# The second layer's first two units: sums of squares and scores placed behind the next projection, the adapters' mean in one piece

## The reference

```python
x = x + tanh(g_xattn[0]) * L0_attention(layernorm(x), ctx)     # rotary, masked, 32 heads, 8 key groups
x = x + tanh(g_ffn[0])   * L0_experts(layernorm(x))            # 16 experts, top 2
x = x + tanh(g_xattn[1]) * L1_attention(layernorm(x), ctx)
x = x + tanh(g_ffn[1])   * L1_lora(layernorm(x))               # 4 adapters, top 2
```

```python
q = rmsnorm(hidden @ Wq.T) * q_norm_w
k = rmsnorm(ctx @ Wk.T) * k_norm_w
probs = softmax(q @ k.T / sqrt(128) + mask)
out = (probs @ v) @ Wo.T
```

## Time and profile before

| | us |
|---|---|
| median of three executions (lowest, highest) | 1195.96 (1195.57, 1196.04) |
| the profiled execution | 1196.31 |
| its span, first to last instruction | 1194.3 |
| TensorE busy | 1181.7 |
| VectorE busy | 829.7 |
| GpSimd busy | 580.6 |
| ScalarE busy | 424.0 |

### The profile page before, as it was taken

One profiled execution on the slowest core, in us unless ns is written; L12 is line 12 of the kernel. 1 busy time (PEld: TensorE's weight loads), 2 busy tenths in 40 slices (PEclk: granted clock), 3 DMA queues, 4 the chain that ended last, 5 costly groups with the idle time before them and its releaser, 6 DMA issues.

```text
span 1194.3 us, 16826 instructions
## 1 busy us (share of the span) xinstructions
PE 1181.7 (99%) x6178; PEld 944.8 (79%) x6178; DVE 829.7 (69%) x1454; ACT 424.0 (36%) x746; POOL 580.6 (49%) x396
## 2 busy tenths in 40 slices
PE   9999999999999999999999999999999999999998
PEld 7888888777777777777788888777777777777776
DVE  4656546888888888788984335766676767657795
ACT  5145152222213222222452124535443443544432
POOL 5522533766767576676463112335354554545500
PEclk9999999999999999999999999999999999999999
DMA  7844635712212221211211003111221221211201
GB/s 282 261 145 167 201 117 161 281 54 80 80 53 72 86 79 44 79 45 45 97 63 36 1 1 138 50 49 71 86 82 44 79 78 54 70 53 40 76 1 72
DMA packets 57314, 106.54 MB, mean 89 GB/s; under 512 B 3632, under 2 KB 36528, under 8 KB 51888
## 3 DMA queue, kind: packets, MB, share of 16 engines
q1 hardware_dynamic: 56736, 104.82, 25.4%
q0 software_dynamic: 384, 1.05, 0.2%
q10 hardware_dynamic: 144, 0.00, 0.0%
HBM read 78.59 MB, written 27.26 MB: 89 GB/s over the span
## 4 chain that ended last, share of the span: by engine, by line
PE 91%; DVE 6%; POOL 2%; issue 1%; ACT 0%; DVEq 0%; POOLq 0%
PE ps_q L225 13%; PE ps_b L225 13%; PE ps_b L227 13%; PE ps_b L226 13%; PE ps_q L227 12%; PE ps_q L226 12%; PE ps_s L935 4%; PE ps_b L962 4%; PE ps_q L922 1%; PE ps_s L273 1%; PE ps_q L2039 1%; PE ps_b L469 1%; PE ps_s L1730 1%; PE ps_q L519 0%; DVE x_sb L1439 0%
## 5 line engine op out<-in xcount | busy, mean ns | idle before, releaser
L225 PE MATMUL ps_q<-hT_hi,wq_hi 128*128 128x512 f32 x512 | 206.3, 403 | 0.0
L226 PE MATMUL ps_q<-hT_lo,wq_hi 128*128 128x512 f32 x512 | 199.8, 390 | 0.0
L227 PE MATMUL ps_q<-hT_hi,wq_lo 128*128 128x512 f32 x512 | 199.4, 389 | 0.0
L225 PE MATMUL ps_b<-wo_hi,o_hi 128*128 128x512 f32 x440 | 171.5, 390 | 0.6 <-POOL wo_lo L1253 0.6
L226 PE MATMUL ps_b<-wo_lo,o_hi 128*128 128x512 f32 x440 | 171.2, 389 | 0.0
L227 PE MATMUL ps_b<-wo_hi,o_lo 128*128 128x512 f32 x440 | 171.2, 389 | 0.0
L1428 DVE TENSOR_TENSOR o_lo<-ps_b,o_hi 128x512 fp32r<-128x512 f32 x128 | 82.0, 683 | 63.7 <-ACT o_hi L1138 62.4
L225 PEld LDWEIGHTS ps_q<-hT_hi,wq_hi 128*128 128x128 f32 x512 | 96.0, 188 | 33.2 <-issue 11.2
L1260 POOL TENSOR_TENSOR qT<-q_t 128x512 f32<-128x512 f32 x64 | 89.7, 1402 | 65.8 <-DVE q_t L1363 60.0
L1439 DVE SCALAR_TENSOR_TENSOR x_sb<-ps_b,gates,x_sb 128x512 f32<-128x512 f32 x117 | 83.8, 723 | 43.6 <-PE ps_b L227 43.2
L728 POOL TENSOR_TENSOR wq_lo<-wq_raw,wq_hi 128x512 fp32r<-128x512 f32 x64 | 90.3, 1414 | 47.8 <-ACT wq_hi L722 47.8
(11 more groups left out here) (272 smaller groups left out, 2474.6 us busy)
## 6 DMA issues: line engine op xcount, KB each, us to landing
wq_raw<-in_wq SPq DMA_DIRECT2D x16, 1024.0 KB, 4.8
wo_raw<-in_wo SPq DMA_DIRECT2D x16, 1024.0 KB, 4.8
kT<-kT_spill SPq DMA_DIRECT2D x32, 256.0 KB, 3.9
v_hi<-v_hi_spill SPq DMA_DIRECT2D x16, 512.0 KB, 3.7
v_lo<-v_lo_spill SPq DMA_DIRECT2D x16, 512.0 KB, 4.6
v_hi_spill<-vs_hi SPq DMA_DIRECT2D x12, 512.0 KB, 5.4
v_lo_spill<-vs_lo SPq DMA_DIRECT2D x12, 512.0 KB, 6.7
kw_raw<-in_wk SPq DMA_DIRECT2D x4, 1024.0 KB, 7.1
```

The costliest lines, as they stand in the source:

```text
L225: nc.tensor.matmul(dst, l_hi, r_hi, start=first, stop=False)
L226: nc.tensor.matmul(dst, l_hi, r_lo, start=False, stop=False)
L227: return nc.tensor.matmul(dst, l_lo, r_hi, start=False, stop=last)
```

## The change

In the second layer's steps (0, 1) and (1, 0) (`opening`), TensorE makes the first projection of the step and only then the sums of squares and the scores of the unit before. In step (0, 1) a wait for the last low part of the layernormed x is put ahead of that projection. `square_sums` of unit 1 thereby moves from the end of step (0, 1) into step (1, 0), behind `project(1, 0, 0)`. The mean of the adapters' weights is made with four matmuls in one piece at the end of step (0, 1). On ScalarE the first query of unit 1 goes ahead of the norms of unit 0. On VectorE the turn of the sums of unit 1 moves from step (0, 1), where it stood ahead of the low part of unit 0's probabilities, to step (1, 0), behind it.

```diff
--- before.py
+++ after.py
@@ -1012,15 +1012,18 @@
                     for t in range(PAIRS):
                         project_out(0, 0, 0, t)
                     return
-                if second_first_scores(lay, g, h):
-                    lora_mean_pe(pe, True)
-                if do_score and lay:
-                    if not (isinstance(g, int) and (g, h) == (1, 0)):
-                        square_sums(us, 1 - h)
+                opening = lay and isinstance(g, int) and (g, h) in ((0, 1), (1, 0))
+                if do_score and lay and not opening:
+                    square_sums(us, 1 - h)
                     score(us, 1 - h, g if h else g - 1)
                 at_first = lay and isinstance(g, int) and (g, h) == (0, 0)
+                if second_first_scores(lay, g, h):
+                    pe.wait_ge(*lns[2]("lo", NT))
                 if do_project:
                     project(g, h, 0)
+                if opening:
+                    square_sums(us, 1 - h)
+                    score(us, 1 - h, g if h else g - 1)
                 if do_score and lay == 0:
                     score(us, 1 - h, g if h else g - 1)
                 if do_project:
@@ -1038,8 +1041,7 @@
                     project(g, h, 3)
                 for t in range(PAIRS):
                     if second_first_scores(lay, g, h) and t == 1:
-                        lora_mean_pe(pe, False)
-                        square_sums(us + 1, 1)
+                        lora_mean_pe(pe)
                     if do_finish:
                         project_out(up, h, g - 1, t)
 
@@ -1172,9 +1174,9 @@
                 if do_finish and h == 0 and not (isinstance(g, int) and g == 1):
                     for j in range(J):
                         wo_high(g - 1, j)
-                query_ahead = do_score and do_project and lay and h == 0 and not (isinstance(g, int) and g == 1)
+                query_ahead = do_score and do_project and lay and (h == 0 or second_first_scores(lay, g, h)) and not (isinstance(g, int) and g == 1)
                 if query_ahead:
-                    queries(uq, 0, 0)
+                    queries(uq, h, 0)
                 if do_score and lay:
                     norms(us)
                 for j in range(J):
@@ -1477,7 +1479,6 @@
                     sums(us)
                     att_normalise(dve, lay, us)
                     turn_probs(us)
-                    turn_sums(us + 1, h)
                     att_probs_low(dve, lay, us)
                     return
                 if lay == 0 and isinstance(g, int) and (g, h) == (0, 0):
@@ -1512,7 +1513,7 @@
                     return
                 rotated(0)
                 if do_score:
-                    if lay and not (isinstance(g, int) and (g, h) == (1, 0)):
+                    if lay:
                         turn_sums(us, 1 - h)
                     turn_scores(us, 1 - h)
                     if lay:
@@ -1998,15 +1999,13 @@
 
             return att[1]("y_added", 2 * (G - 1) * PAIRS + i + 1)
 
-        def lora_mean_pe(pe, first):
-
-            if first:
-                pe.wait_ge(lora["a_in"], 16)
-                pe.wait_ge(moe["gu"], 2 * NT)
-            for k in range(2) if first else range(2, KC):
+        def lora_mean_pe(pe):
+
+            pe.wait_ge(lora["a_in"], 16)
+            pe.wait_ge(moe["gu"], 2 * NT)
+            for k in range(KC):
                 last = nc.tensor.matmul(ps_b[0][:, 0:LN], ones[:, :], a_raw[:, k, :], start=k == 0, stop=k == KC - 1)
-            if not first:
-                last.then_inc(lora["a_sum"], 1)
+            last.then_inc(lora["a_sum"], 1)
 
         def lora_mean_act(act):
```

## The result

The change made the kernel slower: 1203.0 us (median of six executions, 1201.19 to 1203.75) against 1195.64 us for the kernel before (six executions, 1195.24 to 1196.04). The ratio is 1.0058, with a 95% interval of 1.0049 to 1.0068. It is 7.4 us over the kernel before, where the forecast has 5.8 (1201.8 less 1195.96). The profiled execution is the fastest one (1201.19 us, span 1199.4 us); the other five took 1202.56 to 1203.75 us. The mean granted clock over the whole span was 0.999 of full speed in the fastest one and 0.997 in each of the other five.

A forecast was written before the change was run, and what follows sets the result against it. TensorE, busy 1181.7 of 1194.3 us, was taken as the bound. Opening waits put it 4.1 us behind, then 5.8 with the late transpose, giving 1201.8 us from a median of 1195.96; range 1198.7 to 1203.2.

The forecast's parts named there:

- First gap: Before unit 1's first projection: TensorE waits for ScalarE's Copy to free the bank; 0.57 us cost, 1.4 us wait.
- The chain's start: Unit 0's softmax: sums end 3.32 us later, VectorE's eight copies take 1.40 us, transposed scores start 2.9 us later.
- The port: Unit 0's scaling or mask addition on VectorE is held by a GpSimd query-weight subtraction: 1.2 us, bounds 0 and 1.3.
- The exponential and P(2.0): Late exponential delays unit 1's last queries on ScalarE; unit 2's first projection waits 3.3 us, TensorE 4.1 us behind.
- P(2.0) at full rate: Unit 2's first projection, behind the new wait, was taken to run at full clock in 2.75 us.
- the fall of the clock: Rival: after the 3.3 us wait, TensorE drops from 2.4 to 1.2 GHz; 1202.9 or 1205.7 us; chance 0.12.
- The rival's smaller price: Clock-fall rival with only unit 2's first projection slow (5.5 us, 1.7 hidden): 1.1 us more, 1202.9 us.
- The second new wait: Before unit 2's second projection: wait for VectorE's transpose of unit 1's sums, 778.1 to 779.85 us; 5.8 us behind.
- After that: After unit 2's second projection: unit 0's values find probabilities ready; later work shifts 5.5 to 5.9 us, nothing regained.
- Ports shared without waiting: Rival: VectorE and GpSimd operations run together; 3.0 us behind, 1198.9 us; chance 0.20 for sharing in part or whole.
- Bank waits only: Rival: exponential not late for ScalarE, only bank waits cost: 1.1 us, 1197.1 us; chance 0.07.
- Not slower if the bank were another: Rival: without waiting for the Copy, both 0.29 us waits vanish: 1195.4 us; chance 0.05 for a gain or nothing.

The follow-up runs named there:

- no_port: The change with GpSimd's four low-part query-weight subtractions held until unit 0's shift is done: 1201.35 us, 5.5 over the kernel before.
- second_alone: Kernel before with only the second place changed (unit 2's first projection ahead of unit 1's sums and scores; their turn behind probabilities' low part): 1196.66 us, 1.0 over.
- exp_last: The change with unit 0's exponential moved in ScalarE's queue from ahead of unit 1's query 2 to behind query 3: 1203.47 us, 7.6 over the kernel before.
- change_again: The changed kernel itself, unaltered, measured once more as a yardstick: 1202.17 us, 6.5 over the kernel before.
- fill_wait: The change with 12 unread matmuls behind the mean, in TensorE's long wait: 1201.9 us, 6.2 over the kernel before.
- first_alone: Kernel before with only the first place changed (unit 1's first projection ahead of unit 0's sums and scores): 1199.32 us, 3.6 over.
- fill_turn: The change with 12 unread matmuls in TensorE's long wait and VectorE's turn of unit 1's sums back ahead of the probabilities' low part: 1200.17 us, 4.2 over before.
- own_bank_turn: The change with first projections of units 1 and 2 in a free bank and unit 1's sums turned ahead of unit 0's normalisation: 1199.13 us, 3.3 over before.
- own_bank: The change with the first projections of units 1 and 2 put into a free PSUM bank: 1202.45 us, 6.6 over the kernel before.
- bank_second: Kernel before with only the second place changed, its projection in a free bank, sums turned before probabilities' low part, whole mean in first gap: 1194.71 us against 1196.01.

## Why the prediction was right, and where it was not

*First gap.* Predicted: a wait of 1.4 us for the Copy. Measured: 1.36. The transpose of the sums was hidden behind the scores, as stated. The sums were done 5.25 us behind the Square (751.90 to 757.15) against 4.96 predicted: P(1.0) took 2.93 us and not 2.75, and started 0.1 later.

*The chain's start.* The eight copies took 1.43 us (1.40 predicted; 1.79 before).

*The port.* Predicted: 1.2 us, by rows of shorter operations. Measured: 1.07, on the scaling itself, the second of the two orders named. The scaling ended 1.09 us after GpSimd did, and takes 1.23 alone. The Trainium skill's page "SBUF — State Buffer" (section "SBUF: two separate sides") calls the shared port pair an exclusive lock; the trace agrees within 0.14 us. The normalisation was held too, 2.02 us instead of 1.23 (the prediction had it start later and run alone). no_port shows the price by itself; it shows that the two operations do not run side by side, not what they share.

*The exponential and P(2.0).* Predicted 15.7 and 19.5 us behind the Square, with 3.3 us of waiting; measured 15.94, 19.88 and 3.43. second_alone shows that this wait belongs to the first place, exp_last that it is the chain's length and not the exponential's place in ScalarE's queue that costs.

*P(2.0) at full rate: this step failed.* I gave the fall of the clock a chance of 0.12. It fell in the profile of the change and in that of change_again. The first execution's TensorE lost about 1.5 us to it: P(2.0) took 4.37 us (771.78 to 776.15), where P(1.0), also behind a wait, took 2.93, and the sums 0.1 more. The rival's smaller price (P(2.0) alone slow, 1202.9 us) was the nearer one: the median of 1203.0 is that rival's time and not the forecast's 1201.8, and it lies in the range because the range took that price in. Its cover was right as well: the second wait, 1.7 us by the prediction and 1.38 in fill_wait, vanished in the change's trace because the slow matmuls took its place. So P(2.1) started 27.2 us behind the Square against 26.8 predicted, and the profiled execution took 1201.19 us against 1202.1. The other executions, with a mean clock of 0.997 against 0.999, made the median 1203.0. With the clock held up the forecast's own sum is near: fill_wait is 6.2 us over before, against 5.8. What I should have read: the trace of before has no TensorE work behind a wait of this length, so its full clock everywhere was no evidence against the rival, and the Trainium skill's page "TensorE: Matmul & The Clock Gate" (section "What's actually happening"), which says that an idle TensorE falls to 1.2 GHz, was all there was to go by. The traces agree with it for the waits of 3.43, 2.36 and 4.93 us; first_alone's profiled execution kept a clock of 1.00 behind one of 2.75.

*The second new wait* (1.7 us predicted) is shown by fill_wait (1.38) and fill_turn, not by the change's own trace.

*After that.* Nothing was late for the values in the change. own_bank_turn shows that query (2.0), behind p_hi in ScalarE's queue, would have been the next.

*The rivals.* Ports shared without waiting: refuted by the 2.30 us. Bank waits only: refuted by first_alone. Not slower if the bank were another: refuted for both places (own_bank, 6.6 over). For the second place alone it holds in bank_second (0.7 to 1.3 under), where nothing of the chain is delayed, but there the turn of the sums and the mean were moved as well.

About 0.5 us of the opening's 6.2 is in none of these terms: waits grew by 4.2 (1.36 + 3.43 less 2 x 0.29), the clock took 1.5, and the rest is the draining and refilling of TensorE's pipeline around the new waits (P(1.0) took 2.93 us instead of 2.75); that part I only infer.

## What to carry to other kernels

Before work is put ahead of the first link of a long chain over several engines, follow that chain to its users: the delay is paid where the chain is next waited for, here 19 us later and in another step. Moving a link of the late chain within its queue (the exponential, exp_last) only moved the wait; moving an operation that does not need the chain out from behind it (the turn of the sums, fill_turn) took 1.3 us off. A wait that another one hides is still owed: fill_wait took away the visible loss and found the next. And where waits of TensorE grow as here, from 0.29 to 2.36 us and more, price the clock as likely, not as a tail.

## What the hardware did that I had not expected

With waits of 2.4 to 4.9 us ahead TensorE ran for a stretch at the 1.2 GHz level (a granted clock of 0.62 from 772 to 776 us in the change, 0.50 in change_again there and in own_bank from 776 to 780), and 128x512 matmuls then took 0.63 us instead of 0.39. After 2.75 us it did so in the profile of own_bank_turn, not in that of first_alone, and by their mean clocks (0.997 against 1.000) in two of the five executions of first_alone. In all, it fell in six of the seven profiles whose opening has a wait of 2.36 to 4.93 us, and in none of the seven whose longest wait there is 1.38 us or less. When it fell differed between two executions of the same kernel with the same wait of 3.43 us: during the wait in change_again (as in no_port), about 1.2 us after its end in the first profile. Unread matmuls in the wait kept it at 1.00 and made own_bank 2.7 us faster (6.6 to 3.9 over before) although TensorE did more. A VectorE operation of 128x1024 with both inputs in SBUF took 2.30 us beside a GpSimd subtraction of 1.29 and 1.23 without one (no_port): the two hardly overlap.
